# One core, four graph layers: another order of the stages' table in a kernel that runs two batches side by side

## The reference

```python
# L0: attention over neighbours, masked with adj
hidden = features @ w;  e = leaky_relu(hidden @ a1 + (hidden @ a2).T)
h = elu(softmax(where(graph == 0, -1e9, e)) @ hidden)
# L1: three layers L1.0, L1.1, L1.2 of attention and a feed-forward net
agg = softmax(where(mask, leaky_relu(si + sj + b), -inf)) @ x
h = layernorm(x + agg);  x = layernorm(h + gelu(h @ W1 + b1) @ W2 + b2)
# L2: as L0, but each row keeps only the weights that reach its 16th largest
# L3: eight heads of masked attention
out = relu(softmax(where(mask, q @ k.T / sqrt(32), -inf)) @ v) @ Wo
```

## Time and profile before

| | before |
|---|---|
| median of 3 runs (lowest to highest) | 3777.41 us (3774.29 to 3780.37) |
| span of the profiled execution | 3773.6 us, so 3.8 us below the median; no separate time of that execution is given |
| PE, PEld, DVE, ACT, POOL busy | 88%, 68%, 65%, 58%, 20% |
| one half period in the middle of the span | 225.4 us |
| mean granted TensorE clock | 0.969 |

### The profile page before, as it was taken

One profiled execution on the slowest core, in us unless ns is written; L12 is line 12 of the kernel. 1 busy time (PEld: TensorE's weight loads), 2 busy tenths in 40 slices (PEclk: granted clock), 3 DMA queues, 4 the chain that ended last, 5 costly groups with the idle time before them and its releaser, 6 DMA issues.

```text
span 3773.6 us, 60010 instructions
## 1 busy us (share of the span) xinstructions
PE 3307.7 (88%) x18240; PEld 2566.8 (68%) x18240; DVE 2461.5 (65%) x7151; ACT 2196.3 (58%) x4349; POOL 773.1 (20%) x1052
## 2 busy tenths in 40 slices
PE   6689989898999899989998899889989898999866
PEld 4577766766667677666766677677766766667653
DVE  3466676666757666676666767666676666766654
ACT  2256556665565756656665565756656665565623
POOL 1212122121311222121121211222121121211210
PEclk8899999999999999999999999999999999999989
DMA  5000000000000000000000000000000000000000
GB/s 138 1 1 12 7 12 7 7 7 7 12 7 6 7 7 12 8 12 7 7 7 7 12 7 6 7 7 12 7 12 7 1 12 7 12 7 1 1 6 6
DMA packets 39858, 40.24 MB, mean 11 GB/s; under 512 B 7264, under 2 KB 38240, under 8 KB 39520
## 3 DMA queue, kind: packets, MB, share of 16 engines
q1 hardware_dynamic: 31072, 27.68, 2.5%
q0 software_dynamic: 8448, 8.39, 1.5%
HBM read 36.07 MB, written 8.39 MB: 12 GB/s over the span
## 4 chain that ended last, share of the span: by engine, by line
PE 49%; issue 23%; DVE 12%; ACT 12%; POOL 3%; DVEq 0%; DMA 0%; POOLq 0%; ACTq 0%; SPq 0%
PE acc L1210 11%; PE work L1234 9%; PE acc L1248 7%; PE acc L1314 3%; PE work L1151 3%; ACT PT L1044 3%; PE acc L1283 3%; PE acc L1295 2%; POOL rstd L515 2%; PE work L1122 2%; PE work L1263 2%; PE work L1195 2%; ACT L1044 2%; DVE T L697 2%; PE acc L1343 2%
## 5 line engine op out<-in xcount | busy, mean ns | idle before, releaser
L1234 PE MATMUL work<-XT,w_sb 128*128 128x256 f32 x3072 | 732.7, 384 | 36.6 <-DVE XT L821 15.0
L515 POOL TENSOR_TENSOR rstd<-var_eps,minus_half 128x2 f32<-128x2 f32 x320 | 225.2, 704 | 2601.2 <-DVE var_eps L773 2601.0
L1248 PE MATMUL acc<-w_sb,gT 128*128 128x256 f32 x3072 | 724.7, 383 | 0.0
L1234 PEld LDWEIGHTS work<-XT,w_sb 128*128 128x128 f32 x3072 | 557.7, 190 | 168.0 <-ACT gT L1026 35.4
L1248 PEld LDWEIGHTS acc<-w_sb,gT 128*128 128x128 f32 x3072 | 575.7, 192 | 95.7 <-issue 22.8
L1026 ACT ACTIVATE gT<-work,b_sb 128x256 f32<-128x256 f32 x768 | 342.3, 472 | 209.1 <-PE work L1234 201.6
L1210 PE MATMUL acc<-X,PT 128*128 128x256 f32 x1536 | 378.0, 402 | 24.7 <-ACT PT L994 24.1
L1210 PEld LDWEIGHTS acc<-X,PT 128*128 128x128 f32 x1536 | 305.0, 202 | 98.0 <-issue 31.1
L1026 ACT ACT_TABLE_LOAD x198 | 254.0, 1283 | 3.5
L757 DVE COPY PT<-work 128x512 f32<-128x512 f32 x160 | 109.6, 685 | 222.9 <-PE work L1195 221.2
L764 DVE BATCH_NORM_STATS2 stats<-R 128x6 f32<-128x256 f32 x640 | 240.9, 418 | 11.0
(11 more groups left out here) (155 smaller groups left out, 5955.3 us busy)
## 6 DMA issues: line engine op xcount, KB each, us to landing
HX<-in_x SPq DMA_DIRECT2D x16, 512.0 KB, 3.8
pos<-in_adj POOLq DMA_DIRECT2D x16, 512.0 KB, 5.7
out<-X SPq DMA_DIRECT2D x32, 256.0 KB, 2.1
w_sb<-in_L_gnn_W SPq DMA_DIRECT2D x6, 1024.0 KB, 8.6
g_sb<-in_L_gnn_g SPq DMA_DIRECT2D x6, 128.0 KB, 6.5
awr_sb<-in_L_gnn_attn_w SPq DMA_DIRECT2D x2, 256.0 KB, 7.8
c_sb<-in_L_gnn_beta SPq DMA_DIRECT2D x3, 128.0 KB, 4.3
PT<-in_L_gnn_b SPq DMA_DIRECT2D x3, 128.0 KB, 5.8
```

The costliest lines, as they stand in the source:

```text
L515: pool.tensor_tensor(rstd[s][:, half_rows(half)], var_eps[s][:, half_rows(half)], minus_half[:], ALU.pow)\
L1234: last = pe.matmul(u.bank[:, 0:HN], w1_sb[:, l, c, f * P:(f + 1) * P], XT[s][:, c, half * HN:(half + 1) * HN], start=(c == 0), stop=(c == ...
L1248: last = pe.matmul(acc[s][half][:, i, :], gT[s][:, f, i * P:(i + 1) * P], w2_sb[:, l, f, :], start=(f == 0 and i == 0), stop=(f == FC - 1) ...
```

## The change

Only the table changes; each stage keeps its code, and each engine its set of stages (PE 155, ACT 139, DVE 133, POOL 35, SP 3 per half). The stages of one batch stay in an order that its data allow. The table loses five lines, so line numbers of the changed kernel are lower by 5. Two lines of it as they stand and stood:

```diff
@@ -82,60 +82,55 @@
...
-        ("middle", "L0", "v1"), ("ending", "L1.2", "hT0 ha0 sum1 norm1 f100 f101 hT1"),
...
+        ("ending", "L1.2", "ha0 hT0"), ("middle", "L0", "v1"), ("ending", "L1.2", "f100 sum1"),
...
```

## The result

The changed kernel takes 3622.8 us, median of 4 runs (3620.9 to 3630.4), against 3778.9 us before in the same job (3774.3 to 3784.2). The ratio is 0.959, 95% interval 0.957 to 0.960: 156 us faster, where 45 had been forecast and where the range ended at 3678. The span of the profiled execution went from 3773.6 to 3619.0 us, its mean granted clock from 0.969 to 0.959. Two executions of the runs further down, one of 4473.8 us and one of 15631.5 us where the others of the same kernel lie within 7 us, were in a slower state of the chip and are left out of their medians.

A forecast was written before the change was run, and what follows sets the result against it. PE, busy 88% of the span, was taken as the bound. Waits of -4.8 and clock of +1.8 gave -3.0 us per half, times 15 -45: 3732 us, whole range 3678 to 3805.

The forecast's parts named there:

- waits, first stretch: Up to the feed-forward net of L1.0: PE's waits fall from 9.8 to 6.0 us per half, -3.8.
- waits, second stretch, to `sq1`: Up to L3's second scores: POOL's moved `ha1` and `xa0` slow DVE's chain, +1.5 us per half on 4.9.
- waits, heads: In the heads: PE work placed over waits for copies, 5.3 to 2.8 us per half, -2.5.
- waits, behind the heads: Fourth stretch, now 1.1 us: `proj0` no longer waits for `hn0`, but odd copies come later; about 1 counted, change 0.
- PE's busy time (clock): L1.0's softmax: one more slow-clock piece after 3.4 us of wait, +1.8 us per half (bounds 0 and twice that).
- opening and closing, in all: The two ends, driven by one batch's chain whose stages keep their order: 0, bounds 5 us either way.
- rival B: Second stretch: DVE is the bound, POOL's `ha1` and `xa0` block it fully, +3.4 per half, 3783 us; 0.14 together with D.
- A: Clock holds and POOL does no harm: -6.3 us per half, 3683 us; chance 0.17.
- its mark of 220 us: Sign for A: the forecast is wrong if the half is under 220 us; 222.4 was forecast.
- C: Heads: ACT becomes the bound through two added table loads and bunched exponentials, +4.1 us per half, 3839 us; chance 0.19.
- D: Each covered wait only moves to the next stage of that batch, whose chain sets the half: 3777 us; 0.14 with B.

The follow-up runs named there:

- the tail part alone: Kernel before with only the last part (`bc` of L1.2, `rt1` and `pv3` to `v0` of the next batch) in the new order: 3726.6 us.
- the order up to `pv3`: Kernel before with the changed order only for L3's end and L1.2's softmax up to `pv3`: 3740.6 us.
- covering the wait alone: Kernel before with `pv3` put ahead of `proj0` at L3's end, nothing else changed: 3773.5 us.
- the front and tail parts: Front: kernel before with the new order only from L1.2's `hT0` to L2's first `mx0`, 3716.2 us; tail: only from `bc` of L1.2 on, 3726.6 us.
- the second run: Kernel before with only the second part (`f102` of L1.0 to L3's `qk0` and `sx1`) in the new order: 3787.4 us.
- the heads' run: Kernel before with only the third part (L3's first scores up to `uT30`, with L1.1) in the new order: 3736.6 us.

## Why the prediction was wrong

The direction was right and its mechanism too: PE's idle time is what moved. The sizes were not, and two terms had been put at nothing. Per half:

| term | forecast | measured |
|---|---|---|
| waits, first stretch | -3.8 | -4.6 |
| waits, second stretch, to `sq1` | +1.5 | -0.05 (+1.27 and -1.32) |
| waits, heads | -2.5 | -2.1 |
| waits, behind the heads | 0 | -1.6 |
| PE's busy time (clock) | +1.8 | -0.3 |
| half | -3.0 | -8.6 |
| opening and closing, in all | 0 | -26 |

- **First stretch and heads: right within 0.8.** The wait at L0's `pT0` is gone as worked out; that at L1.0's `pT0` grew to 3.4 in five halves of 14 and by 1.2 on average, not by 1.7. The terms listed for the first stretch add up to -3.2, not to the -3.8 that stands there, so the sum came nearer to the measured -4.6 than its terms do. The placing of matmuls over the copies of the heads did what it said.
- **POOL's price was about right where it acts.** +1.27 up to the idle transposes against +1.5; moved back, the three stages take 1.9 us of waits away where 2.4 had been put down for two. Beside POOL, DVE kept 0.45 to 0.48 of its speed (0.42 of 0.94, 0.73 of 1.53), where the prediction took 0.57 (0.68 of 1.20) and rival B nothing. What was missed: the idle time behind them (1.32) fell to nothing, because the low clock stretched that very work to 9.64 us busy. Together this place is 0.8 us longer (9.64 against 8.89), and moving the POOL stages back removed it. In all the three stages cost 44 us, 2.9 per half. Missed as well: the rest of the second part's order wins some 25 to 32 us (the two differences above), about 2 us per half, where 0.9 had been counted.
- **"Fourth stretch: 0" was the first wrong step.** It measured -1.6 of waits (-1.9 with PE's busy time), and -2.5 with the tail part alone. I had priced the covered wait (1.11) against what was put ahead of the odd copies, and had not asked when L1.2's softmax starts. The runs show 2.2 us per half from the order up to `pv3`, in which that start lies, and that covering the wait alone gives nothing per half.
- **"Clock +1.8" was the second.** The low clock did grow, and by more than forecast: it lasts 13.8 us per half instead of 8.3, and PE's busy time in it went from 7.6 to 12.9 us. As groups take about twice as long there, half of the difference, 2.7 us, is its cost in busy time (my estimate). But a low piece was charged to the half in full. It was free where a wait of PE for another engine followed, and 2.8 us were lost where it came behind one. And PE's busy time did not grow, since the waits became fewer, 16.8 per half instead of 28.1, and a group behind a wait is itself longer (1.36 us against 1.04 for 8 transposes, and the rows around them); the term left this out.
- **"The ends: 0, their order is kept" was the third, 26 us.** The rows of the two ends give PE's idle time from 83.5 to 74.6 in the opening and from 27.6 to 21.3 in the closing, its busy time 5.2 and 5.5 less with the clock at 0.90 and 0.97 instead of 0.89 and 0.92. Alone, the front and tail parts shorten the opening by 8.2 and 6.9 us, the heads and tail parts the closing by 5.4 and 3.5. So the order within one batch's own stages matters where it runs alone; by which stages, no run shows.

Of the rivals, A had the right sign of error and was still 60 us short, and its two reasons do not hold: the low clock lasts longer, and POOL did 44 us of harm. That the half fell below its mark of 220 us is luck for A. B, C and D are refuted by the second run, the heads' run and the result. ACT's table loads rose as forecast. Before:

```profile
L1026 ACT ACT_TABLE_LOAD x198 | 254.0, 1283 | 3.5
L1044 ACT ACT_TABLE_LOAD x75 | 96.2, 1283 | 1.3
```

After:

```profile
L1021 ACT ACT_TABLE_LOAD x228 | 292.5, 1283 | 4.0
L1039 ACT ACT_TABLE_LOAD x90 | 115.5, 1283 | 1.6
```

These two lines and the 15 more at the line of the softmax's exponentials (63 to 78) are the 60 loads, 77 us of ACT. PE did not wait for them: its waits for Gelu's results fell from 1.3 to 0.7 us per half.

The Trainium skill ("ScalarE: Activation LUTs", What ACT_TABLE_LOAD costs) gives about 2.66 us for a switch, about 1.28 of them the load itself and the rest a drain. Each load here shows 1.283, as the page has it; the drain does not show, neither behind the load (Gelu starts 1.29 after it began) nor ahead of it (4.0 us idle ahead of 228 loads).

The Trainium skill ("SBUF — State Buffer", Who interferes with whom) says that a DVE instruction with two SBUF inputs contends with a GpSimd instruction that reads SBUF, for a port pair that one of them holds exclusively. The trace agrees in kind: the dot product, which has two inputs, takes 0.94 us instead of 0.42 beside POOL's additions, and these are slowed too. The norms have one tensor input and two columns of scalars, and lose 0.80 us a pair. The section lets such an instruction contend if it runs in a 2-port mode; no row here tells in which mode the norms ran.

## What to carry to other kernels

Where an order of stages is changed, do not price a covered wait by its own length: ask which chain of the other batch it ends, and when that chain starts. Behind the heads the gain came with an earlier start of that chain, and the same wait covered without it only moved. Keep POOL's long elementwise stages out of the times in which DVE runs a chain that PE waits for, even if POOL's own results are early enough anywhere: three such stages were 44 us here, as much as the forecast gain of the whole change.

## What was not expected of the hardware

The mean granted clock and the time do not go together: 0.959 at 3622.8 us and 0.971 at 3622.1, and the kernel before had 0.969 at 3778.9. In the two halves shown above, what counted was whether the slow matmuls stood ahead of a wait for another engine or behind it.

In six halves, every second one, the kernel before (a turn of the loop is two halves) has a gap in the middle of L0's `v0` in which PE waits for nothing that the profile shows:

```profile
2010.95 1.98 PE L1151 MATMUL work<-w_sb,XT 128*128 128x258 f32 x8
2014.61 2.00 PE L1151 MATMUL work<-w_sb,XT 128*128 128x258 f32 x8 [1.67 <-issue]
```

It is 1.6 to 2.3 us in the kernel before. In the changed one it is 0.4 to 0.6 in five halves, with 0.7 to 1.3 more in a wait for ACT's copy behind it. I did not test what of it is the loop.

Open is also why the low clock begins where it does. In the rows shown it begins behind or near waits of PE, and it differs from half to half with the same order of work, but no run here separates what starts it.
